# Nine places reordered in a fused attention and feed-forward block: gram by halves, code loads and weight decoding ahead

## What is computed

```
y      = layernorm(x)                       # over the 1024
scores = einsum('lnc,lmc->lnm', y, y)/sqrt(512)   # a 4 x 4 gram for each column l
prob   = softmax(scores); msg = einsum('lnm,lmc->lnc', prob, y)
x1     = x + y + msg
xn     = layernorm(x1)
g, u   = xn @ Wg.T, xn @ Wu.T               # 1024 -> 3584
out    = x1 + (silu(g) * u) @ Wd.T          # 3584 -> 1024
```

## Time and profile before

| | |
|---|---|
| time, median of 3 runs | 1668.82 us (1667.91 to 1668.83) |
| profiled execution, its own time | 1667.4 us |
| its span, first to last instruction | 1665.7 us |
| PE busy | 1630.1 us (98%) |
| DVE busy | 1202.4 us (72%) |
| ACT busy | 1030.1 us (62%) |
| POOL busy | 59.8 us (4%) |
| mean granted TensorE clock | 0.998 of full |

### The profile page before, as it was taken

How to read it: one execution, slowest core, us unless ns; L and a number is a source line. 1 busy time by engine, 2 the same in 40 slices (tenths; PEclk the granted TensorE clock), 3 DMA queues, 4 the chain that set the end, 5 groups by cost and what they waited for, 6 DMA issues and landing times.

```text
span 1665.7 us, 20171 instructions
## 1 busy us (share of the span) xinstructions
PE 1630.1 (98%) x7888; PEld 786.5 (47%) x7888; DVE 1202.4 (72%) x1540; ACT 1030.1 (62%) x1118; POOL 59.8 (4%) x98
## 2 busy tenths in 40 slices
PE   6889999999999999999999999999899999999999
PEld 6865444444444444444444444444344444444444
DVE  7888967685766767576686767678777767577566
ACT  5679676776766667676666767688786526352000
POOL 4261000000000000000000000000000000000000
PEclk9999999999999999999999999999999999999999
DMA  6340232331422233142233314243764444343773
GB/s 269 114 165 14 95 120 95 120 139 52 161 91 104 95 121 139 51 164 95 96 103 112 140 51 165 95 151 100 258 249 176 150 150 175 125 175 126 254 258 123
DMA packets 76895, 226.39 MB, mean 136 GB/s; under 512 B 5248, under 2 KB 19968, under 8 KB 76288
## 3 DMA queue, kind: packets, MB, share of 16 engines
q1 hardware_dynamic: 76800, 225.10, 37.7%
HBM read 156.93 MB, written 68.16 MB: 135 GB/s over the span
## 4 chain that ended last, share of the span: by engine, by line
PE 93%; DVE 3%; ACT 2%; issue 1%; DMA 1%; POOL 0%; SPq 0%; DVEq 0%; POOLq 0%
PE ps L1553 20%; PE ps L1555 20%; PE ps L1554 20%; PE ps L1691 10%; PE ps L1692 10%; PE ps L1693 10%; PE ps L1523 2%; DVE stats L938 1%; PE ps L1532 1%; ACT codes L641 1%; PE ps L1509 0%; DMA codes<-q_dram 0%; DMA xa<-x_dram 0%; ACT xa L691 0%; POOL ln_scale L572 0%
## 5 line engine op out<-in xcount | busy, mean ns | idle before, releaser
L641 ACT ACTIVATE codes<-codes 128x1024 f32<-128x1024 f32 (+1 forms) x672 | 708.1, 1055 | 153.8 <-DMA codes<-q_dram 139.9
L1386 DVE SCALAR_TENSOR_TENSOR xb<-ps,y_back,xb 128x512 f32<-128x512 f32 x140 | 103.9, 749 | 73.5 <-PE ps L1693 68.9
L1553 PE MATMUL ps<-xa,wg 128*128 128x512 f16 x388 | 147.0, 379 | 1.1 <-issue 1.1
L1553 PE MATMUL ps<-xb,rw 128*128 128x512 f16 x388 | 147.1, 379 | 0.7 <-ACT gs L723 0.7
L1553 PE MATMUL ps<-xa,rw 128*128 128x512 f16 x388 | 147.1, 379 | 0.0
L1554 PE MATMUL ps<-xa,rw 128*128 128x512 f16 x388 | 147.1, 379 | 0.0
L1555 PE MATMUL ps<-xa,rw 128*128 128x512 f16 x388 | 147.1, 379 | 0.0
L1553 PE MATMUL ps<-xb,wg 128*128 128x512 f16 x388 | 147.1, 379 | 0.0
L1554 PE MATMUL ps<-xb,wg 128*128 128x512 f16 x388 | 147.1, 379 | 0.0
L1555 PE MATMUL ps<-xb,wg 128*128 128x512 f16 x388 | 147.1, 379 | 0.0
L1554 PE MATMUL ps<-xb,rw 128*128 128x512 f16 x388 | 147.1, 379 | 0.0
(11 more groups left out here) (278 smaller groups left out, 2914.3 us busy)
## 6 DMA issues: line engine op xcount, KB each, us to landing
codes<-q_dram SPq DMA_DIRECT2D x84, 512.0 KB, 4.6
absm<-a_dram SPq DMA_DIRECT2D x69, 512.0 KB, 3.7
h_dram<-rw SPq DMA_DIRECT2D x28, 1024.0 KB, 4.2
gs<-h_dram SPq DMA_DIRECT2D x21, 1344.0 KB, 5.9
h_dram<-rw SPq DMA_DIRECT2D x28, 768.0 KB, 4.6
rw<-h_dram SPq DMA_DIRECT2D x11, 896.0 KB, 5.8
rw<-x_dram SPq DMA_DIRECT2D x16, 512.0 KB, 11.0
xa<-a_dram SPq DMA_DIRECT2D x13, 512.0 KB, 5.4
```

The source lines that it names most:

```text
L641: fn(real, real if step else whole, ACT.Prelu, bias=at0, scale=slope, alpha=left).then_inc(bends_done, 1)
L1386: return v.scalar_tensor_tensor(out=dst, in0=ps[:, bank, :], scalar=y_back[:, 0:1], in1=dst, op0=ALU.mult, op1=ALU.add)
L1553: mm(dst, w_hi, x_hi, start=(start and kt == 0), stop=False, skip_group_check=True)
```

## The change

- **Gram by halves.** The gram of c = 0 and of c = 1 is done in two halves of the blocks. For c = 0 the first half of batches 2 and 3 is normalized by DVE with (x - mean) * scale (`y_first_halves`), which needs only POOL's power (`root_first`), the second half by ACT; POOL does none of c = 0. For c = 1 ACT and POOL write by halves.
- **Exponential ahead.** `exp_half(0)` stands ahead of the last bend of job 1 and of `w_high(0)`; on DVE, `over_sum(0)` to `less_max(1)` stand ahead of the seven small operations; PE does three `transpose_y` groups, not two, ahead of `repeat_prob(0)`.
- **Three message banks** (2, 3, 4) from k = 8 on.
- **x tiles by column halves.** Tile k is column half k // 4 % 2 and batch k % 4, and `half` waits for four tiles before each first multiply and for the other four before the second.
- **Codes ahead of h.** In unit 0 of the down stage SP issues `load_h(2)` and then `load_after(60)`; `load_h(3)` comes after it. Four bends of job 61 (`AHEAD`) are done before unit 0's first take; `STEPS` ends with 0 in place of 4.
- **Last bank in two.** In the last unit, bank b7 becomes two halves of 256 columns in PSUM banks 0 and 1; DVE finishes and SP stores each by itself.

```diff
-STEPS = (6, 3, 6, 3, 6, 6, 6, 4)
+STEPS = (6, 3, 6, 3, 6, 6, 6, 0)
+AHEAD = 4
...
+        def message_bank(k):
+            return 2 + (k % 2 if k < LG else (k - LG) % 3)
...
             for v in range(NV):
-                if v == 1:
+                if v in (2, 4):
+                    store_h(SLOTS - 3 + v // 2)
+                if v == 0:
                     load_h(v + 2)
-                elif v in (2, 4):
-                    store_h(SLOTS - 3 + v // 2)
-                if v in UNIT_OF_JOB:
+                    load_after(DOWN_JOBS)
+                elif v in UNIT_OF_JOB and v > 1:
                     load_after(UNIT_OF_JOB[v])
-                if v in (0, 2, 3, 4, 5):
+                if 1 <= v < 6:
                     load_h(v + 2)
...
-            bends(1)
+            bends(1, range(0, NB - 1))
+            exp_half(0)
+            bends(1, range(NB - 1, NB))
             w_high(0)
-            exp_half(0)
...
             bends(DOWN_JOBS, range(4, NB))
+            bends(DOWN_JOBS + 1, range(0, AHEAD))
...
-            at = 0
+            at = AHEAD
             for t in range(UNITS):
...
+            def y_first_halves():
+                dve.wait_ge(root_first, 2)
+                for n in range(2, B):
+                    v.tensor_scalar(y_nat[0][:, 0:LB // 2, n, :], acc[0][:, n, 0:L // 2].rearrange("p (b l) -> p b l", l=32),
+                                    mean_var[:, 0, n, 0:1], ln_scale[:, 0, n:n + 1],
+                                    ALU.subtract, ALU.mult).then_inc(y_dve, 1)
...
+            over_sum(0)
+            mask_gram(1)
+            turn_prob(0)
+            spread_prob(0)
+            sum_gram(1)
+            less_max(1)
             dve.wait_ge(norm_root, 1)
...
-                c, n, f = k // 8, k // 2 % B, k % 2
+                c, f, n = k // 8, k // B % 2, k % B
...
+                pe.wait_ge(xlo_done, order + B)
                 multiply(mat, A11, first, at, True)
...
+                pe.wait_ge(xlo_done, order + 2 * B)
                 multiply(mat, A12, second, at, False)
...
-                if k >= 2:
+                if k >= LG + 2:
+                    pe.wait_ge(x1_ready, k - 2)
+                elif k >= 2:
                     pe.wait_ge(x1_ready, k - 1)
...
-            for g in range(2):
+            for g in range(3):
                 transpose_y(0, g)
             repeat_prob(0)
...
+                    for f in range(2):
+                        part = row[:, 1, 256 * f:256 * f + 256]
+                        dve.wait_ge(d3_done, t + 1 + f)
+                        v.scalar_tensor_tensor(out=part, in0=last_halves[:, f, :], scalar=y_minus[:, 0:1], in1=part,
+                                               op0=ALU.mult, op1=ALU.add).then_inc(final, 1)
```

More of the change, by code:

```diff
@@ L483, in store_out @@
             def store_out(u):
+                if u == UNITS - 1:
+                    store_last()
+                    return
                 for half in (1, 0):
@@ L487, in store_out, with store_last @@
                                  x1_buf[u % 4][:, 2 * half:2 * half + 2, :]).then_inc(out_done, 16)
+            def store_last():
+                u = UNITS - 1
+                row, to = x1_buf[u % 4], [out_v[ORDER[2 * (u // B) + half], u % B] for half in range(2)]
+                sp.wait_ge(final, 4 * u + 2)
+                sp.dma_start(to[0][:, 0:512], row[:, 0, :]).then_inc(out_done, 16)
+                sp.wait_ge(final, 4 * u + 3)
+                sp.dma_start(to[1].rearrange("p (e t) -> p e t", e=2), row[:, 2:4, :]).then_inc(out_done, 16)
+                sp.wait_ge(final, 4 * u + 4)
+                sp.dma_start(to[0][:, 512:768], row[:, 1, 0:256]).then_inc(out_done, 16)
+                sp.wait_ge(final, 4 * u + 5)
+                sp.dma_start(to[0][:, 768:1024], row[:, 1, 256:512]).then_inc(out_done, 16)
             load_after(UP_JOBS)
@@ L652, in y_rows, with y_halves @@
                        bias=ln_bias[:, c % 2, n:n + 1], scale=ln_scale[:, c % 2, n:n + 1]).then_inc(y_act, 1)
+            def y_halves(c, f, rows):
+                act.wait_ge(ln_ready, c + 1)
+                for n in rows:
+                    fn(y_nat[c][:, half_lb(f), n, :], acc[c][:, n, 512 * f:512 * f + 512].rearrange("p (b l) -> p b l", l=32),
+                       ACT.Identity, bias=ln_bias[:, c, n:n + 1], scale=ln_scale[:, c, n:n + 1]).then_inc(y_act, 1)
             def copy_yt(c, g):
@@ L767, in w_high @@
                 fn(w, tmp[:, 0:4, :].rearrange("p b t -> p (b t)"), ACT.Copy, bias=0.0, scale=1.0).then_inc(whi_done, 1)
-            for c in range(CT - 1):
-                y_rows(c)
+            y_rows(0)
+            y_halves(0, 1, range(2, B))
+            y_halves(1, 0, range(0, 2))
+            y_halves(1, 1, range(0, 2))
+            y_rows(2)
             bends(0, range(0, 4))
@@ L1051, in _ @@
                     row_stats(c, half)
-                    if half == 2 and c:
+                    if c == 0 and half == 3:
+                        row_sums(0, range(2))
+                    elif c == 1 and half == 0:
+                        y_first_halves()
+                    elif c > 1 and half == 2:
                         y_row(c - 1)
-                    elif half == 3 and not c:
-                        row_sums(0, range(2))
                 row_sums(c, range(0 if c else 2, B))
@@ L1564, in half @@
                 mat, unit, later = HALVES[j]
+                order = 16 * unit + 8 * later
                 first = x12 if later else xt[unit][:, X11, :, :, :, :]
@@ L1693, in down, with down_half @@
                     last = mm(ps[:, bank, :], h_lo, w_hi, start=False, stop=ends, skip_group_check=True)
+                return last
+            def down_half(a, b, f, start):
+                pairs = list(enumerate(GROUPS[-1]))
+                mem = h_mem[h_slot(NV - 1)[0]]
+                for at, i in pairs:
+                    h = mem[at].bitcast(F16).rearrange("p (b s t) -> p b s t", b=7, s=2)
+                    h_hi, h_lo = h[:, a, 0, :], h[:, a, 1, :]
+                    w_hi, w_lo = wd[i][:, f, 0, b, :], wd[i][:, f, 1, b, :]
+                    ends = at == len(pairs) - 1
+                    mm(last_halves[:, f, :], h_hi, w_hi, start=(start and at == 0), stop=False, skip_group_check=True)
+                    mm(last_halves[:, f, :], h_hi, w_lo, start=False, stop=False, skip_group_check=True)
+                    last = mm(last_halves[:, f, :], h_lo, w_hi, start=False, stop=ends, skip_group_check=True)
                 return last
```

139 lines of the change are left out of this document (84 added, 55 removed).

## The result

| | before | after |
|---|---|---|
| time, median of the runs made together | 1668.37 us | 1688.68 us (1686.86 to 1689.18, 4 runs) |
| profiled execution, its own time | 1667.4 | 1686.9 |
| its span | 1665.7 | 1685.1 |

The changed kernel takes 1.0119 times as long, 95% interval 1.0107 to 1.0132: 20 us slower. The forecast was 1683.0 us with a range of 1675 to 1693.

The account below looks back on a forecast made before the run. PE, busy 98% of the span, was taken as the bound, so only its idle time counted. Terms +15.4 + 2.1 - 1.6 - 1.1 + 0.6 - 1.2 = +14.2 us gave 1681.6, or 1683.0 against the median; range 1675 to 1693.

Parts of the forecast that it names:

- down units: First eight down units: four PE stalls behind late codes, plus half clock, less old waits removed; +15.4 us.
- end: Kernel end: last DVE operation on half the columns and a smaller last store; -1.2 us, bounds -1.5 and +0.2.
- I take 5.3 where an h load is under way: Down units: codes of jobs 62 and 63 land 5.3 us after issue, against 4.7 with no h load.
- ACT is in time there: Down unit 2: ACT's takes do not delay PE; fourth product ends at 1176.7, adds at 1177.6.
- Front: Before the third message: longer DVE chain, later repeated probabilities, half clock; third message starts +2.1 us later.
- Messages: Message stage: the third bank removes PE's gaps of 0.94 and 0.70 us; -1.6 us.
- The 1.1 us wait goes, -1.1: First half: waiting for four tiles instead of eight removes PE's 1.1 us wait; -1.1 us.
- The joined gap: Second half: gaps of 2.4 and 0.97 us join into one of 3.4; 0.6 of 1.7 us clock loss, +0.6.
- one of 2.45 was not: Second half: a gap of 2.82 us was followed by half clock, one of 2.45 us was not.
- Codes in time: Rival, down units: early load means ACT never blocks, 7.7 us saved, total about 1660 us; chance 0.09.
- Only the first stall: Rival, down units: later loads are in time, -0.6 us there, total about 1667 us; chance 0.06.
- Landing slow everywhere: Rival, down units: every codes load takes 7.1 us, +25 us there, total 1693 us; chance 0.12.

Follow-up runs that it names:

- e8: Kernel before with only the three message banks and the last bank in two: 1665.86 us, ratio to before 0.9985.
- e11: Kernel before with x tiles by column halves, and half 1 waiting once more for the low half's x tiles: 1668.98 us, ratio 1.0001.
- e7: Kernel before with only the x tiles by column halves and half's waits for four tiles each: 1670.18 us, ratio 1.0008.
- e1: Kernel before with only the SP order changed, codes of job 62 loaded ahead of the h of unit 3: 1661.78 us, ratio 0.9957.
- e2: Changed kernel with the four bends ahead taken back (AHEAD 0, STEPS ending in 4), all other edits kept: 1663.02 us, ratio to before 0.9962.
- e5: Kernel before with only the gram by halves for c = 0 and c = 1: 1669.68 us, ratio 1.0006.
- e6: Kernel before with only the exponential ahead (ACT, DVE and PE order around the first probabilities): 1669.60 us, ratio 1.0008.
- e10: Kernel before with SP order, four bends ahead with first bends left in place, three message banks, last bank in two: 1657.61 us, ratio 0.9936.
- e9: Changed kernel with DVE's scaling ahead of h's sums and the first two codes loads ahead of the h loads on SP: 1680.04 us, ratio to before 1.0067.
- e4: Changed kernel with DVE's scaling and block sums of jobs 60 and 61 ahead of h's sums: 1689.29 us, ratio to before 1.0121.

## Why the prediction was right, point by point

The mechanism was the one forecast. Its size was forecast too small: 1683.0 us was said and 1688.7 measured, that is +14.2 us against about +20. What it named as evidence is there: four waits for ACT's take, the longest over 5 us; ACT waiting for codes in units 0, 2, 4 and 5; half clock after three; no wait for the down weights; `over_sum(0)` at 47.3 and `repeat_prob(0)` at 50.6 us; one gap over 3 us near 125. Term by term on the profiled execution (+19.4 on the span, +14.2 forecast):

| term | forecast | measured | read from |
|---|---|---|---|
| down units | +15.4 | +18.0 | end of the last matmul +20.56, less +2.5 at 1143 us |
| all before 1143 us | 0.0 | +2.5 | PE's matmul behind the same copy at 1143.37, before at 1140.86 |
| end | -1.2 | -1.15 | 2.7 us after the last matmul, before 3.9 |

**The stalls, mis-sized.** Forecast 5.4, 6.5, 4.4 and 1.5 us; measured 6.1, 7.4, 4.9 and 1.3, 1.9 us more in all. Two steps were too short. The first is "I take 5.3 where an h load is under way": the two such loads took 6.2 and 5.6 us, 0.9 and 0.3 more. The second is "ACT is in time there" for unit 2, and the adds of unit 4 in the same way: the adds waited for ACT's first take, behind three bends, and ended about 1 us later than forecast. Measured to the point where the take was due, this made the requests for jobs 63 and 64 about 0.8 and 0.5 us late. The third stall's excess comes from this alone, as its codes took the forecast 4.7 us. The clock cost three times 1.7 in the forecast, less the 1.7 of before: 3.4. Idle time explains 19.7 - 6.0 = 13.7 of the 18.0, so the clock took about 4.3, which is 2.0 for each stall. 1.7 came from one stretch at half clock, and the stretch after the first stall here lasts 4.7 us at 1.2 GHz, a loss of half of that, 2.3.

**The rule and the trace.** The rule of the Trainium skill that the prediction cites, strict first-in first-out queues on ACT (TensorE: Matmul & The Clock Gate, Part 1, engine queue depths), held in each case: the take at 1166.78 started only when the bend that had waited 7.28 us had been issued.

**Front, right.** The second `repeat_prob`, with the third message behind it, starts at 60.05 and before at 58.07, +2.0 for a forecast +2.1, with a 4.3 us gap and half clock behind it as forecast. Part of the agreement is luck. The same start lies at 58.1, 58.3, 58.7 and 59.0 us in e8, e11, e7 and e1, where the front is that of the kernel before, and at 60.7 in e2. The kernel before has half clock behind its 2.8 us gap as well, from about 51.1 to 54.5 us, only later. And what ends last ahead of 60.05 is DVE's division, for which PE waits 1.36 us.

**Messages, right.** The waits of 0.94 and 0.70 us are gone, in e8 alone as well. One of 0.2 us at 84.70 is new.

**The first half, a step that failed.** "The 1.1 us wait goes, -1.1": it does, but in its place PE waits 1.15 us at 111.09 for ACT's copy of a tile, so the term is 0. PE's start at 128.7 us is the same as before (128.71 and 128.79). The forecast had said itself that this start is fixed by ACT and DVE; a wait of PE alone that goes ahead of it could then not be added to the sum. What moves ACT and DVE as well does count there: in e8, where the messages end sooner, PE's wait of 2.4 us ends at 119.12 and before at 121.16.

**The joined gap, mis-sized.** It is 3.6 us (forecast 3.4) and the clock did halve; the forecast gave this 0.6 of 1.7 us. The whole 1.7 us are lost, since no wait follows that could take them up, and a wait of 1.02 us at 155.82, for DVE's part of a tile, stands where 0.3 stood; the prediction has no term for it. Together they are the +2.5. Both stand in e7's rows too, so they belong to the x tiles, though e7's time shows only 1.3 us of them, with an interval up to 2.8. Part of that difference may be the trace of the kernel before: its clock stayed at 1.00 after the gap of 2.45 us, which the forecast took for a property of the gap ("one of 2.45 was not"). In e5, e6, e8 and e10 the same gap was followed by half clock. Where it was, PE's work past 128.8 us came 0.5 us later, so against such an execution the +2.5 are about 2.0.

**The end, right.** DVE's last operation took 0.48 us (forecast 0.42), 0.27 less than before. The last store took 1.8 us, 0.8 less than the 512 KB one; the forecast had 1.0, from a data part of "about 1.35" that no row shows. The matmuls of 256 columns follow each other every 0.11 us, so the doubled count cost nothing. These make 1.07 of the 1.15 us.

**The rivals.** "Codes in time" (faster) would have needed codes by 1156; they landed at 1165.8. "Only the first stall" needed DVE ahead in unit 2; its scaling came at 1184.96, after unit 2's adds, as argued against it. "Landing slow everywhere" has a small share in it: the two loads beside h took 6.2 and 5.6 us, between the 5.3 taken and the 7.1 of that case, and the other two 4.7 and 4.6.

## What to carry to other kernels

When work of a list is moved earlier, look for the item of the list that waits for a transfer: it moves too, and in a queue in program order all that stands behind it waits as well. Here the same four operations cost 25 us slid forward with the list and gained about 1 us, by the wait that they shortened, with the first bends left in place. A load's request is as early as the latest of what it waits for and what stands ahead of it in its queue, so an edit of one of these alone may be worth nothing. And a wait of PE alone that goes ahead of a start that another engine fixes doesn't count, while a slow stretch of PE ahead of such a start costs less than it lasts: joining two gaps moved the slow stretch to where nothing takes it up. Before a difference of 1 us is put down to the clock, read the clock over the whole stretch, and in more than one trace.

## What the runs showed of the hardware

- The granted clock after a gap of PE, in this kernel: 1.00 after one of 1.9 us (e9), 0.50 after 3.6, 4.3, 4.6, 4.9, 5.9, 6.1 and 7.4 us. In between it was not the same in every trace: the same gap of 2.4 us was followed by 1.00 in the kernel before and e1, and by 0.50 in e5, e6, e8, e10 and e11 (for e11 0.58 over 121 to 125 us). After the 2.8 us gap of the kernel before, the clock was at 1.00 for about 1.5 us and then at 0.50.
- The stretch at half clock was not of one length: about 4.7 us after the 6.1 us gap, 3.9 after the 7.4 us one, 2.8 after the 4.9 us one, and 6 us in e9 after its second stall (1189.6 to about 1195.6 us), ahead of which stood a gap of 5.9 us.
- 512 KB of codes landed 4.6 us after their issue in e9 when the h load was started 0.9 us behind them, and after 5.6 to 6.5 us where one had been started 0.9 to 2.2 us ahead (the changed kernel and e4). With an h load 0.6 us behind they took 4.6 to 4.8 us five times and 5.8 and 6.0 us once each (the changed kernel, e4 and e9), so the place of the h load alone doesn't set it.
- Stores to memory at the end of the kernel, on SP's queue: 1.8 us for the last one of 128 KB, 2.0 for 256 KB and 2.6 for 512 KB. The Trainium skill (DMA: Bandwidth & Descriptors, Anatomy of one DMA) fits 2.0 us and the bytes over 436 GB/s, measured on the GpSimd path; that makes 2.3, 2.6 and 3.2 us for 128, 256 and 512 KB. The slope is seen between 256 and 512 KB here (0.6 us), but on SP's queue the fixed part is smaller: an estimate of 1.4 us from the two larger stores.
